# Adding the experts' sum bank by bank and first in the step, with the last block stored in halves

## The reference, cut to what matters

```python
h = h + attn(layernorm(h))
# ffn: 16 routed experts (4 chosen for a token) and a shared part of two further experts' size
hid = relu2(einsum('th,eih->eti', flat, W1))     # up
y = einsum('eti,ehi->eth', hid, W2)              # down
out = einsum('eth,te->th', y, cw)                # cw: routing weights, zero for experts not chosen
shared = relu2(flat @ Ws1.T) @ Ws2.T
h = h + (out + shared)
```

## Time and profile before

| what | value |
|---|---|
| median of 3 runs | 1342.09 us (1340.52 to 1342.47) |
| the profiled execution | 1341.05 us, of which the span is 1339.3 us |
| PE, PEld busy | 1228.9 us (92%), 1020.1 us (76%) |
| DVE busy | 1067.7 us (80%) |
| ACT, POOL busy | 630.1 us (47%), 524.8 us (39%) |
| mean share of the DMA engines | below three tenths in all 40 slices after the first |
| granted PE clock | full in every slice from the fifth on |

### The profile page before, as it was taken

The page is one execution under the profiler, slowest core; times in us unless marked ns, Lnnn a source line. Parts: engine busy times, 40 slices in busy tenths (PEclk is TensorE's granted clock), DMA queues, the critical chain, the costliest instruction groups (busy, mean ns, idle before and its releaser), DMA issues.

```text
span 1339.3 us, 19873 instructions
## 1 busy us (share of the span) xinstructions
PE 1228.9 (92%) x7488; PEld 1020.1 (76%) x7488; DVE 1067.7 (80%) x1726; ACT 630.1 (47%) x1072; POOL 524.8 (39%) x723
## 2 busy tenths in 40 slices
PE   1755999999999999999999999999999999999998
PEld 0342887878787887878788787878878788887887
DVE  1667979798897979889797988889797888979653
ACT  2144354545545454554545454454545445454443
POOL 6261535336063533516253451625344161514100
PEclk9867999999999999999999999999999999999999
DMA  3021112212121222212122221212122122212121
GB/s 116 0 83 60 63 48 80 80 65 79 49 80 47 81 79 65 79 49 80 49 95 63 73 71 49 80 59 85 64 80 64 60 72 73 67 48 80 64 95 64
DMA packets 34128, 91.66 MB, mean 68 GB/s; under 512 B 4720, under 2 KB 13296, under 8 KB 34032
## 3 DMA queue, kind: packets, MB, share of 16 engines
q1 hardware_dynamic: 30960, 81.99, 18.2%
q0 software_dynamic: 3072, 8.39, 2.5%
HBM read 81.46 MB, written 8.91 MB: 67 GB/s over the span
## 4 chain that ended last, share of the span: by engine, by line
DVE 45%; PE 28%; ACT 10%; issue 10%; POOL 4%; DVEq 2%; DMA 1%; ACTq 0%; POOLq 0%; SPq 0%
DVE hid_lo L663 10%; PE psB L932 8%; DVE ring L692 7%; PE psY L905 7%; PE psH L890 6%; DVE r_sb L658 6%; DVE ring L300 4%; PE psA L973 4%; DVEq L741 2%; DVE ring L320 2%; ACT p_sb L522 2%; DVE o_sb L327 2%; DVE stats L675 2%; ACT hid_hi L524 2%; ACT L598 1%
## 5 line engine op out<-in xcount | busy, mean ns | idle before, releaser
L905 PE MATMUL psY<-w_hi,hid_hi 128*128 128x256 f32 x1152 | 327.4, 284 | 21.4 <-DVE h L669 21.4
L522 ACT ACTIVATE p_sb<-r_sb 128x512 f32<-128x512 f32 x288 | 180.9, 628 | 346.8 <-DVE r_sb L658 345.7
L905 PE MATMUL psY<-w_lo,hid_hi 128*128 128x256 f32 x1152 | 323.5, 281 | 0.0
L905 PE MATMUL psY<-w_hi,hid_lo 128*128 128x256 f32 x1152 | 323.2, 281 | 0.0
L905 PEld LDWEIGHTS psY<-w_hi,hid_hi 128*128 128x128 f32 x1152 | 216.8, 188 | 50.2 <-issue 39.2
L663 DVE TENSOR_TENSOR hid_lo<-p_sb,hid_hi 128x512 fp32r<-128x512 f32 x288 | 232.7, 812 | 27.2 <-ACT hid_hi L524 26.8
L890 PE MATMUL psH<-xT_hi,w_hi 128*128 128x512 f32 x576 | 233.8, 406 | 0.0
L890 PE MATMUL psH<-xT_lo,w_hi 128*128 128x512 f32 x576 | 228.3, 396 | 0.0
L890 PE MATMUL psH<-xT_hi,w_lo 128*128 128x512 f32 x576 | 228.2, 396 | 0.0
L905 PEld LDWEIGHTS psY<-w_lo,hid_hi 128*128 128x128 f32 x1152 | 216.8, 188 | 11.0
L320 POOL TENSOR_TENSOR ring<-ring 128x512 f32<-128x512 f32 x96 | 126.6, 1318 | 239.6 <-DVE ring L692 239.6
(11 more groups left out here) (132 smaller groups left out, 1977.8 us busy)
## 6 DMA issues: line engine op xcount, KB each, us to landing
cwB<-cw_dram SPq DMA_DIRECT2D x128, 512.0 KB, 3.8
out<-h SPq DMA_DIRECT2D x32, 256.0 KB, 3.2
h<-w_t SPq DMA_DIRECT2D x3, 512.0 KB, 3.9
xin<-table,idx POOLq DMA_INDIRECT x64, 3.8
p_sb<-w_t SPq DMA_DIRECT2D x4, 256.0 KB, 4.2
cwB<-w_t SPq DMA_DIRECT2D x4, 256.0 KB, 3.4
ring<-wqkv_t SPq DMA_DIRECT2D x2, 384.0 KB, 3.3
cwB<-w_t SPq DMA_DIRECT2D x1, 512.0 KB, 3.8
```

What stands on the lines that cost most here:

```text
L522: nc.scalar.activation(p_sb[:, n % 2, :], r_sb[:, n % 2, :], ACT.Square)
L905: last = nc.tensor.matmul(psY[:, j // 2, (j % 2) * D:(j % 2 + 1) * D], hid[a][:, e % R, j * P:(j + 1) * P], W2[b][:, e, :], start=(e == 0 ...
```

## The change

`add_experts` is split in two instructions of 128 x 512, one for each bank of `psY`. Both move to the head of step e = 0, ahead of `weigh(n + 2)` and `hidden_lo(n + 1)`. Half 0 waits for a new semaphore `y_half_mm`, which PE raises when j = 1 of the block's last expert is done; half 1 waits for the whole of it (`w2_mm`). `y_added` now counts halves: PE's first `down` of a block waits for half 0 ahead of j = 0 and for half 1 ahead of j = 2. SP stores blocks 0 to 14 as before, after both halves; the last block is stored in four DMAs, two as soon as half 0 is added and two after half 1.

```diff
@@ SP, block_io
-                sp.wait_ge(y_added, nth(blk, 1, 2))
                 par = blk % 2
-                for q in range(2):
-                    sp.dma_start(out_v[q, bass.ds(blk, 1), :, :, :]...,
-                                 h1[par][q * NN:(q + 1) * NN, :, :]).then_inc(out_stored, 16)
-                sp.wait_ge(out_stored, nth(blk, 32, 32))
+                if blk < B - 1:
+                    sp.wait_ge(y_added, nth(blk, 2, 4))
+                    ... (the same two DMAs and wait)
+                else:
+                    for half in range(2):
+                        sp.wait_ge(y_added, nth(blk, 2, 3 + half))
+                        js = slice(2 * half, 2 * half + 2)
+                        for q in range(2):
+                            sp.dma_start(out_v[q, bass.ds(blk, 1), :, js, :]...,
+                                         h1[par][q * NN:(q + 1) * NN, js, :]).then_inc(out_stored, 16)
+                    sp.wait_ge(out_stored, nth(blk, 32, 64))
@@ DVE
-            def add_experts(blk):
+            def add_experts(blk, half):
                 par = blk % 2
-                dve.wait_ge(w2_mm, nth(blk, X_ALL, X_ALL))
-                nc.vector.tensor_tensor(h1[par] (128 x 1024), psY (both banks), h1[par], ALU.add).then_inc(y_added, 1)
+                if half == 0:
+                    dve.wait_ge(y_half_mm, nth(blk, 1, 1))
+                else:
+                    dve.wait_ge(w2_mm, nth(blk, X_ALL, X_ALL))
+                h = h1[par][:, 2 * half:2 * half + 2, :].rearrange("p j d -> p (j d)")
+                nc.vector.tensor_tensor(h, psY[:, half, :], h, ALU.add).then_inc(y_added, 1)
@@ DVE, step_of
+                if e == 0 and blk > 0:
+                    add_experts(blk - 1, 0)
+                    add_experts(blk - 1, 1)
                 if n + 2 < B * X_ALL:
                     weigh(n + 2)
                 if n + 1 < B * X_ALL:
                     hidden_lo(n + 1)
-                if e == 0 and blk > 0:
-                    add_experts(blk - 1)
@@ PE, down
-                if e == 0:
-                    pe.wait_ge(y_added, nth(blk, 1, 1))
                 for j in range(TT):
+                    if e == 0 and j % 2 == 0:
+                        pe.wait_ge(y_added, nth(blk, 2, 1 + j // 2))
                     for a, b in PASSES:
                         ...
+                    if e == X_ALL - 1 and j == 1:
+                        last.then_inc(y_half_mm, 1)
```

More of the change, by code:

```diff
@@ L197, in lm_tower_layer @@
         w2_mm = sem("w2_mm")
+        y_half_mm = sem("y_half_mm")
         y_added = sem("y_added")
@@ L378, in block_io @@
                     weights_io(att)
-                sp.wait_ge(y_added, nth(blk, 1, 2))
                 par = blk % 2
-                for q in range(2):
-                    sp.dma_start(out_v[q, bass.ds(blk, 1), :, :, :].rearrange("o n j d -> (o n) j d"),
-                                 h1[par][q * NN:(q + 1) * NN, :, :]).then_inc(out_stored, 16)
-                sp.wait_ge(out_stored, nth(blk, 32, 32))
+                if blk < B - 1:
+                    sp.wait_ge(y_added, nth(blk, 2, 4))
+                    for q in range(2):
+                        sp.dma_start(out_v[q, bass.ds(blk, 1), :, :, :].rearrange("o n j d -> (o n) j d"),
+                                     h1[par][q * NN:(q + 1) * NN, :, :]).then_inc(out_stored, 16)
+                    sp.wait_ge(out_stored, nth(blk, 32, 32))
+                else:
+                    for half in range(2):
+                        sp.wait_ge(y_added, nth(blk, 2, 3 + half))
+                        js = slice(2 * half, 2 * half + 2)
+                        for q in range(2):
+                            sp.dma_start(out_v[q, bass.ds(blk, 1), :, js, :].rearrange("o n j d -> (o n) j d"),
+                                         h1[par][q * NN:(q + 1) * NN, js, :]).then_inc(out_stored, 16)
+                    sp.wait_ge(out_stored, nth(blk, 32, 64))
                 sp.sem_inc(h1_free, 1)
@@ L640, in _ @@
         def _(dve):
-            dve.sem_inc(y_added, 1)
+            dve.sem_inc(y_added, 2)
             def weight_lo(k):
@@ L664, in hidden_lo @@
                                         hid[0][:, n % R, :].bitcast(f32), ALU.subtract).then_inc(hid_lo, 1)
-            def add_experts(blk):
+            def add_experts(blk, half):
                 par = blk % 2
-                dve.wait_ge(w2_mm, nth(blk, X_ALL, X_ALL))
-                nc.vector.tensor_tensor(h1[par][:, :, :].rearrange("p j d -> p (j d)"),
-                                        psY[:, :, :].rearrange("p a t -> p (a t)"),
-                                        h1[par][:, :, :].rearrange("p j d -> p (j d)"), ALU.add).then_inc(y_added, 1)
+                if half == 0:
[4 more added lines that the diff above has]
+                nc.vector.tensor_tensor(h, psY[:, half, :], h, ALU.add).then_inc(y_added, 1)
             def norm_stats(w, blk, src):
@@ L872, in _ @@
                     step_of(b, e)
-            add_experts(B - 1)
+            add_experts(B - 1, 0)
+            add_experts(B - 1, 1)
         @block.tensor
```

## The result

| | before | after |
|---|---|---|
| median | 1340.24 us (20 runs, 1338.83 to 1343.21) | 1342.84 us (20 runs, 1340.64 to 1345.58) |
| ratio to before | 1 | 1.0018, 95% interval 1.0010 to 1.0025 |
| span of the profiled execution | 1339.3 us | 1338.9 us |

The change makes the kernel 0.18% slower, 2.4 us (by the ratio; the two medians are 2.6 apart). I had forecast 1.1 us less than before. I compare stretch by stretch.

What follows compares the result with a forecast made beforehand. DVE was taken to bound the stretches with PE's stalls, PE the last block; +0.1 - 0.24 - 0.95 = -1.1 us gave 1341.0 us from the median 1342.09, range 1337.5 to 1344.5.

Steps and rivals of the forecast that it cites:

- no change: Whole kernel: a difference within 0.2%, or 2.7 us, can't be told from none; chance 0.74.
- the last blocks: Last block's first down, where PE sets the pace: its wait for the add goes, -0.24 us (bounds 0 and -0.24).
- the exchange with POOL: Head of 14 blocks: later hidden_lo meets other POOL adds, +0.01 us a block; rivals: it costs 0.09, gains 0.10.
- the end: After the last matmul: only the second half's data is left to store, -0.95 us (bounds 0 and -1.25).
- What bounds the kernel: PE's 14 stalls, 21.4 us, lie where DVE sets the pace, so removing them gains nothing; rival that PE bounds: 0.04.
- The split: Head of 14 blocks: two adds take 1.20 us instead of one of 1.13, costing 0.07 a block (bounds 0 and 0.15).
- ACT's squares: Head of a block: ACT's two squares wait for weigh, 1.20 us later, but delay nothing: 0.
- the cover of 2.1 us: Head of a block: time from weigh's end to the hidden_lo needing ACT's squares; any excess would add to each block.
- The figure of 0.6: Last stores: saving for 256 KB less by the skill's 436 GB/s, an estimate beside the forecast's -0.95 us.

Runs made afterwards that it cites:

- split only: Changed kernel with the two adds of 128 x 512 back behind weigh and hidden_lo, last block added after all its matmuls: 1338.77 us, 1.0000 of before.
- pair with POOL cut: Kernel before and changed kernel, both with POOL's first two adds cut to one column in 64 in two position sums per block: 1326.14 and 1325.69 us.
- Order only: Kernel before with its one add of 128 x 1024 moved unsplit to the head of the step, last block as before: 1346.04 us, 1.0053 of before.
- delays of four and eleven: Kernel before with four or eleven unused BATCH_NORM_STATS instructions added on DVE in block 9: 1343.03 us (1.0021) and 1343.06 us (1.0023).
- delay of eight: Changed kernel with eight unused BATCH_NORM_STATS instructions added on DVE in one block: 1346.35 us, 1.0039 of before.
- quarters: Changed kernel with each half of the add cut in two, four adds of 128 x 256 at the head of the step: 1341.28 us, 1.0012 of before.
- between: Changed kernel with the head of a block reordered to weigh, half 0, hidden_lo, half 1: 1330.89 us, 0.9940 of before.

## Why the prediction was wrong where it was

The measured 1342.84 us lies inside the range, and 0.18% inside what I called no change; but the sum had the wrong sign: -1.1 us forecast, +2.4 measured, +1.5 by the traces. Of the 2.6 us between forecast and traces the last blocks make 1.7, the exchange with POOL 0.7 and the end 0.2. That the time fell inside the range is no merit of the sum: the range is 7 us wide, and the forecast started from a median of 3 runs, 1342.09, that came out as 1340.24 over 20. By its steps:

- *What bounds the kernel*: right. PE's 21.4 us of stall were worth nothing; after the change PE waits some 16.5 us more elsewhere, for L704 in front of L979 and L936 and, a little, for `xT_lo`. That PE's lead ends at the transposes, at the latest, was right too.
- *The split, +0.07 a block*: the size was right (1.20 us against 1.13), but it does not show: split only costs 0.01 a block, since the `hidden_lo` behind it waits for POOL in either case.
- *The exchange with POOL*: the mechanism was right in each instruction, and the Trainium skill's rule ("SBUF — State Buffer", Who interferes with whom) agrees with every row shown: the later one waits for the whole instruction. The rows also bear out what the rule was cited for, that this speaks against the move. The term was mis-sized: +0.01 a block forecast, +0.10 measured. Counted from the head of the step, the 0.09 are L321's start 0.01 later, its 1.29 us instead of 1.26, and the end of the second `hidden_lo`, 0.60 us behind the end of L323 (836.04 to 836.64) where I had taken 0.55. I took the forecast as exact to 0.01 by agreement with one row; a chain of four hand-overs isn't.
- *ACT's squares, 0*: the cover of 2.1 us, from the end of `weigh`, held in the real kernel (833.82 to 835.96). The pair with POOL cut shows what the squares need: 1.18 us, and DVE was back after 1.12.
- *The last blocks, -0.24*: this is the step that failed. The stall in front of the last block's first `down` did go (1.42 us on the chain). But "here PE sets the pace" took PE's pace as given, and it is not: 3.4 us more at half clock, worth 1.7 us, were spent 25 us earlier. So the term came out as +1.5 and not -0.24. I had read the granted clock of the page as full from the fifth slice on and had not looked at what the 0.91 between 1250 and 1270 us hung on.
- *The end, -0.95*: right, -0.8. The last DMA is issued no earlier, as worked out, and only its data are less. The figure of 0.6, an estimate from the Trainium skill ("DMA: Bandwidth & Descriptors", Anatomy of one DMA), lies on the other side of the 0.8. That section is on DMAs that GpSimd issues, and these are issued by SP, so no more than the size can be compared.

With what the traces show the sum is +0.8, +1.5 and -0.8. Order only, without the gain at the end and with the clock's fall 1.26 us ahead of the transposes, is the same change at its worst.

*The clock.* Shown, in traces: the loss of clock comes with a delay alone, with DVE's order untouched; it does not grow with the delay (four instructions 13.7 us, eleven 6.8); and over 13 traces, one of each kernel and two of the changed one, it goes with one number, where PE stands when the clock falls. PE idles 3.25 us in front of block 15's transposes in every kernel while POOL ends the statistics and ACT normalises. If the transposes have begun when the clock falls, 3.4 us run at half clock; if they have not, 6.8 or 13.7. Against the fall the transposes start 0.79 us later in the changed kernel's trace than in that of before (from 0.21 ahead of it to 0.58 behind it), and the 0.10 us of each block is more than enough for that.

Not shown: that the position of the fall is the cause and not a companion (the delays of four and eleven lost clock as foretold, but the one kernel that was to lose less, the delay of eight, lost more); what decides between 6.8 and 13.7; and that each timed run behaves as its kernel's one trace. The added lengths of the traces of five complete kernels lie outside the measured intervals: order only just below, quarters and the three delays above. The mean clocks over the runs (0.9762, 0.9746, 0.9732) speak for it only on average, and part of them comes from other parts of the run. How the changed kernel would run without the loss of clock was not tried.

## What to carry to other kernels

An engine's wait is worth money only where it lies on the chain: 14 stalls of 1.5 us on the busiest engine, all of them in a stretch that DVE set, were removed for nothing. Where DVE's instructions with two SBUF inputs meet POOL's adds, try to move instructions that read PSUM into the time of POOL's long ones and to put the two-input ones where POOL is between two: the same six instructions took 4.62, 4.54 (split only) or 3.91 us by their order alone. And before one trusts a difference of one or two us, one looks at the granted clock of both traces near every idle time of PE.

## What the runs showed of the hardware

- A DVE instruction of 128 x 512 with two SBUF inputs ends 0.55 us behind the POOL add that it waits for; a POOL add of 128 x 256 ends 0.60 us behind the DVE instruction that it waits for (both in the traces of before and of the change). DVE instructions with one PSUM and one SBUF input kept their 0.68 us (128 x 512) and 1.21 to 1.23 us (128 x 1024) beside POOL in every trace shown.
- In eight of the 13 traces the fall of the clock nearest to block 15's transposes comes 1201.5 us after the run's first one, though the kernels differ; in the others it is 1184.4 (before with POOL cut), 1191.3 (changed with POOL cut), 1198.1 (between), and 1204.9 twice (the kernel before with eleven instructions of delay, the changed one with eight). Where PE's idle time stands against it differs by tenths of a microsecond from kernel to kernel (the table above).
- Two DMAs of 128 KB instead of 256 KB behind the last add end the kernel 0.8 us earlier though the last one is issued at the same time, each issue taking SP 0.63 us.
